# The modular stage of an eleven-stage kernel, rewritten for two batches in the two halves of the array

## The reference, cut to what matters

```python
h = h + _L2_ffn_ref(_layernorm(h, axis=-1), ...)

def _L2_ffn_ref(x, attention_mask, wr, br, w1, b1, w2, b2):
    weights = (jnp.einsum('bsd,do->bso', x, wr) + br)[..., 0]
    k = max(1, int(CAPACITY * s))          # CAPACITY = 0.5
    kk = k - 1 if k > 1 else 1             # 123 of 249 tokens
    _, idx = jax.lax.top_k(weights, k)
    sel_idx = idx[:, :kk]
    sel = take(x, sel_idx)
    h = gelu(sel @ w1 + b1)                # 64 -> 256
    y = (h @ w2 + b2) * w_sel              # 256 -> 64
    return zeros.at[sel_idx].set(y) + x
```

## Time and profile before

| | us |
|---|---|
| median of three runs | 6294.06 |
| the three runs | 6295.24, 6255.51, 6294.06 |
| profiled execution | 6266.99 |
| its span, first to last instruction | 6265.2 |
| PE busy in it | 5338.2 (85%) |
| DVE busy | 3326.5 (53%) |
| ACT busy | 2326.1 (37%) |
| POOL busy | 1796.3 (29%) |
| mean granted PE clock | 0.790 |

### The profile page before, as it was taken

The page is one execution under the profiler, slowest core; times in us unless marked ns, Lnnn a source line. Parts: engine busy times, 40 slices in busy tenths (PEclk is TensorE's granted clock), DMA queues, the critical chain, the costliest instruction groups (busy, mean ns, idle before and its releaser), DMA issues. The chain is left out here.

```text
span 6265.2 us, 119967 instructions
## 1 busy us (share of the span) xinstructions
PE 5338.2 (85%) x34237; PEld 3582.2 (57%) x34237; DVE 3326.5 (53%) x9404; ACT 2326.1 (37%) x5857; POOL 1796.3 (29%) x1988
## 2 busy tenths in 40 slices
PE   4429995677799799997999667887999999979999
PEld 4416663555455466665666564554666666646665
DVE  1245553444455456563444344665777777754554
ACT  3313332000000023333444231113777777755555
POOL 0002221111000134342222472002444444433333
PEclk9997776555555578898999655556999999989999
DMA  0011001111111101013333111110000000013332
GB/s 9 6 36 23 20 21 16 40 39 41 27 25 25 25 20 24 24 25 66 81 81 78 34 42 31 26 27 22 11 10 10 10 10 10 9 28 71 73 73 63
DMA packets 523064, 205.84 MB, mean 33 GB/s; under 512 B 491532, under 2 KB 514044, under 8 KB 522748
## 3 DMA queue, kind: packets, MB, share of 16 engines
q1 hardware_dynamic: 522876, 203.78, 14.7%
HBM read 157.78 MB, written 45.91 MB: 33 GB/s over the span
## 5 line engine op out<-in xcount | busy, mean ns | idle before, releaser
L3026 POOL TENSOR_TENSOR att_P<-att_P,att_rden 125x498 f32<-125x498 f32 x512 | 520.2, 1016 | 640.5 <-DVE att_rden L3297 640.5
L3213 ACT ACTIVATE att_P<-att_pS,att_nb 125x249 f32<-125x249 f32 x1024 | 471.7, 475 | 17.5 <-DVE att_nb L3305 17.5
L2417 DVE TENSOR_TENSOR moe_hT<-moe_silu,moe_pH 128x498 f32<-128x498 f32 x384 | 258.7, 674 | 324.8 <-ACT moe_silu L2403 324.8
L3634 ACT ACTIVATE sw_hT<-sw_pH,sw_b 128x498 f32<-128x498 f32 x512 | 317.9, 672 | 243.2 <-PE sw_pH L3588 243.2
L3129 PEld LDWEIGHTS att_pP<-att_ident,att_P 124*125 124x125 f32 (+1 forms) x2048 | 262.4, 187 | 187.9 <-issue 187.9
L3129 PE MATMUL att_pP<-att_ident,att_P 124*125 124x124 f32 (+1 forms) x2048 | 351.9, 294 | 10.1 <-POOL att_P L3026 8.7
L3305 DVE TENSOR_REDUCE att_nb<-att_pS 125x2 f32<-125x498 f32 x512 | 322.4, 667 | 46.6 <-PE att_pS L3117 45.0
L3220 ACT ACTIVATE att_PTr<-att_pP 125x498 f32<-125x498 f32 x512 | 304.4, 594 | 92.5 <-PE att_pP L3129 86.5
L2403 ACT ACTIVATE moe_silu<-moe_pH 128x498 f32<-128x498 f32 x384 | 225.1, 586 | 285.0 <-PE moe_pH L2360 199.1
L1023 PE MATMUL att_pS<-att_kT,att_qT 16*125 16x249 f32 x1024 | 302.1, 477 | 2.1 <-ACT att_kT L1129 1.3
L3588 PE MATMUL sw_pH<-sw_xT,sw_w 64*128 64x249 f32 x2048 | 286.2, 398 | 0.0
(11 more groups left out here) (456 smaller groups left out, 12609.2 us busy)
## 6 DMA issues: line engine op xcount, KB each, us to landing
moe_share<-mixing SPq DMA_DIRECT2D x64, 498.0 KB
sw_share<-mixing SPq DMA_DIRECT2D x64, 498.0 KB
att_F<-h_stream SPq DMA_DIRECT2D x192, 62.5 KB
att_X<-h_stream SPq DMA_DIRECT2D x192, 62.5 KB
ffn_w<-in_w1b SPq DMA_DIRECT2D x128, 32.5 KB
ffn_w<-in_L_ffn_W SPq DMA_DIRECT2D x128, 32.0 KB
h_stream<-att_H SPq DMA_DIRECT2D x64, 62.5 KB
ffn_F<-h_stream SPq DMA_DIRECT2D x64, 62.5 KB
```

The lines of the kernel that those rows point to most:

```text
L3026: g.tensor_tensor(own, own, bc(rden[:, j % 2, c, :], T), ALU.mult).then_inc(*scaled.one())
L3213: ins = a.activation(P[:, r, c, t, :], pS[:, 2 * r + c, t * T:(t + 1) * T], ACT.Exp, bias=nb[:, r, c, t:t + 1], accum_out=den[:, r, c, t:t ...
L3634: a.activation(hT[:, k % 4, :, :], pH[:, place, :, 0:T], ACT.Relu, bias=b1[:, k:k + 1]).then_inc(*hid_ready.one())
```

## The change

The stage is written anew.

- **Halves.** A pair's two batches lie in partitions 0 to 63 and 64 to 127 (`xT` is 128 x 249). The products with `wr` and `w1` are one matmul for each batch, 64 rows and 249 columns, each in its half of the rows, into different PSUM banks. Two transposes of 128 columns replace four of 64.
- **Second weights still.** `w2` is the stationary operand (128 x 64), `hT` moves (249 columns), and each batch writes its half of the output partitions. The output has channels in the rows, so ACT copies it out with the bias (`yT`), and PE turns it back with two transposes.
- **Biases.** They are added by ACT (`br`, `b1`, `b2`); the ones row and the bias matmuls go.
- **Own weights.** Four transposes of one row and 125 columns of `W` put each token's own weight in its row; DVE copies them out in one instruction.
- **Ranks.** One DVE pass per group, (W - own) > ties, where ties is -tiny for earlier tokens and 0 otherwise, replaces two; one instruction instead of three forms the gate.
- **Normalisation** is `HalfNorm`, POOL adds `xn` and X (`base`) and the result to it (`H1`).
- **Order.** `waves` with three parts (`pre`, `proj`, `main`) and four steps in place of `pipelined`; SP uses `streamed`. There are ten constant transfers instead of eight.

```diff
-        f = Front(st)
...
+        norm = HalfNorm(st, bodies=WAVES)
...
+                streamed(sp, ahead, keep, store, 4)
...
+                def pre(n, u, step):
+                    if step == 0:
+                        g.wait_ge(*xn_ready.before(n))
+                        norm.center(g, n, g4(Fi[:, u, :, :, :]))
+                        norm.square(g, n)
+                    if step == 2:
+                        norm.power(g, n)
+                    if step == 3:
+                        if since(n, 2):
+                            g.wait_ge(*xT_done.after(n - 2))
+                            g.wait_ge(*base_ready.after(n - 2))
+                        norm.scale(g, n, g4(xn[:, u, :, :, :])).then_inc(*xn_ready.one())
+
+                def main(n, u, step):
+                    if step == 1:
+                        g.wait_ge(*kept.after(n, u))
+                        g.wait_ge(*xn_ready.after(n))
+                        g.wait_ge(*h_ready.before(n))
+                        g.tensor_tensor(base[:, :, :], g4(X[:, u, :, :, :]), g4(xn[:, u, :, :, :]), ALU.add).then_inc(
+                            *base_ready.one())
+                    if step == 3:
+                        g.wait_ge(*res_ready.after(n))
+                        g.wait_ge(*base_ready.after(n))
+                        g.wait_ge(*stored.lagging(n, u))
+                        st.held(g)
+                        g.tensor_tensor(g4(H1[:, u, :, :, :]), res[:, :, :], base[:, :, :], ALU.add).then_inc(
+                            *h_ready.one())
...
-                    pe.matmul(pW[:, 0:2 * T], wr[:, :], f.xT[:, u, :, :], start=True, stop=True).then_inc(
-                        *w_done.one())
-                    for k in range(2):
-                        pe.matmul(pH[:, k, 0:2 * T], w1[:, k * 128:(k + 1) * 128], f.xT[:, u, :, :], start=True,
-                                  stop=True).then_inc(*hid_done.one())
...
+                def proj(n, u, step):
                     if step == 0:
...
+                        pe.wait_ge(*xn_ready.after(n))
+                        pe.wait_ge(*xT_ready.before(n))
+                        st.held(pe)
+                        for t in range(2):
+                            ins = pe.transpose(pX[:, t * OFF:t * OFF + ROWS[t]],
+                                               xn[0:ROWS[t], u, t, :, :].rearrange("p b c -> p (b c)"),
+                                               ident[0:ROWS[t], 0:ROWS[t]])
...
+                    if step == 1:
+                        pe.wait_ge(*xT_ready.after(n))
+                        pe.wait_ge(*w_ready.before(n))
+                        pe.wait_ge(*hid_ready.before(n))
...
+                            r = slice(b * C, (b + 1) * C)
+                            ins = pe.matmul(pW[:, b, 0:T], wr[r, :], xT[r, :], start=True, stop=True)
...
+                        for k in range(2):
+                            for b in range(2):
+                                r = slice(b * C, (b + 1) * C)
+                                ins = pe.matmul(pH[:, b, k * T:(k + 1) * T], w1[r, k * 128:(k + 1) * 128], xT[r, :],
+                                                start=True, stop=True)
...
+                def main(n, u, step):
+                    if step == 0:
+                        pe.wait_ge(*w_ready.after(n))
...
+                                ins = pe.transpose(pN[:, g:g + 1], W[0:1, u, b, t * OFF:t * OFF + PT],
+                                                   ident[0:1, 0:1])
...
+                    if step == 1:
+                        pe.wait_ge(*hid_ready.after(n))
+                        pe.wait_ge(*yT_ready.before(n))
...
+                                ins = pe.matmul(pY[b * C:(b + 1) * C, 0:T], w2[:, k, :], hT[:, u, k, b, :],
+                                                start=(k == 0), stop=(k == 1))
...
+                    if step == 2:
+                        pe.wait_ge(*yT_ready.after(n))
...
+                            ins = pe.transpose(pT[:, t * 128:(t + 1) * 128], yT[:, t * OFF:t * OFF + PT], ident[:, :])
...
+                waves(pe, (lambda n, u, step: None, proj, main), STEPS)
...
+                        a.activation(xT[:, :], pX[:, 0:T], ACT.Copy).then_inc(*xT_ready.one())
...
+                        a.activation(W[:, u, :, :], pW[:, :, 0:T], ACT.Identity, bias=br[:, 0:1]).then_inc(
+                            *w_ready.one())
...
+                            ins = a.activation(hT[:, u, k, :, :], pH[:, :, k * T:(k + 1) * T], ACT.Gelu_apprx_tanh,
+                                               bias=b1[:, k:k + 1])
...
+                        a.activation(yT[:, :], pY[:, 0:T], ACT.Identity, bias=b2[:, 0:1]).then_inc(*yT_ready.one())
...
+                        v.tensor_copy(wn[:, :, :].rearrange("p t b -> p (t b)"), pN[:, 0:4]).then_inc(*n_ready.one())
...
+                                v.scalar_tensor_tensor(out=junk[:, b, :], in0=W[:, u, b, :], scalar=wn[:, t, b:b + 1],
+                                                       in1=ties[:, t, :], op0=ALU.subtract, op1=ALU.is_gt,
+                                                       accum_out=count[:, t, b:b + 1]).then_inc(*counted.one())
...
+                        v.scalar_tensor_tensor(gate[:, :], count[:, :, :].rearrange("p t b -> p (t b)"), float(KEEP),
+                                               wn[:, :, :].rearrange("p t b -> p (t b)"), ALU.is_lt,
+                                               ALU.mult).then_inc(*gate_ready.one())
...
+                        v.wait_ge(*turned.after(n))
+                        v.wait_ge(*h_ready.before(n))
+                        v.tensor_tensor(res[:, :, :], pT[:, 0:256].rearrange("p (g c) -> p g c", g=4),
+                                        bc(gate[:, :], C), ALU.mult).then_inc(*res_ready.one())
```

More of the change, by code:

```diff
@@ L2799, in _, with store @@
+                def store(n, u):
+                    sp.wait_ge(*h_ready.after(n))
+                    st.held(sp)
+                    for ins in store_pair(sp, h, H1[:, u, :, :, :], n):
+                        ins.then_inc(*stored.one(u))
+                streamed(sp, ahead, keep, store, 4)
+                for n in (PAIRS - 2, PAIRS - 1):
+                    sp.wait_ge(*stored.after(n, n % 2))
             @block.gpsimd
             def _(g):
-                g.wait_ge(*f.memset_done.after(0))
@@ L2803, in front @@
[L2803 to L2808, removed]
+                g.wait_ge(*memset_done.after(0))
+                def pre(n, u, step):
[10 more added lines that the diff above has]
+                        norm.scale(g, n, g4(xn[:, u, :, :, :])).then_inc(*xn_ready.one())
@@ L2827, in main @@
-                def main(n, u, ahead):
-                    pe.wait_ge(*hid_ready.after(n))
-                    pe.wait_ge(*y_used.before(n))
-                    st.held(pe)
-                    for t in range(2):
-                        for b in range(2):
-                            g = 2 * t + b
-                            pe.matmul(pY[:, g, :], ones[:, :], b2[:, :], start=True, stop=False)
-                            for k in range(2):
-                                ins = pe.matmul(pY[:, g, :], hT[:, u, k, b * T + t * OFF:b * T + t * OFF + PT],
-                                                w2[:, k, :], start=False, stop=(k == 1))
-                    ins.then_inc(*y_done.one())
-                    ahead(0)
-                    ahead(1)
@@ L2859, in _, with main @@
+                def main(n, u, step):
+                    if step == 1:
+                        a.wait_ge(*y_done.after(n))
+                        a.wait_ge(*turned.before(n))
+                        a.activation(yT[:, :], pY[:, 0:T], ACT.Identity, bias=b2[:, 0:1]).then_inc(*yT_ready.one())
+                waves(a, (lambda n, u, step: None, proj, main), STEPS)
             @block.vector
             def _(v):
-                v.memset(ones[:, :], 1.0)
-                f.memsets(v)
-                v.wait_ge(*f.memset_done.after(0))
@@ L2904, in _, with pre @@
-                pipelined(v, front, main, steps=2)
+                v.memset(norm.expo[:, :], -0.5).then_inc(*memset_done.one())
+                v.wait_ge(*const_loaded.after(0))
+                v.wait_ge(*memset_done.after(0))
+                def pre(n, u, step):
+                    if step == 0:
+                        v.wait_ge(*loaded.after(n, u))
+                        norm.sums(v, n, g4(Fi[:, u, :, :, :]))
+                    if step == 2:
+                        norm.spread(v, n, 1e-5)
@@ L2907, in stage_attention3 @@
+                waves(v, (pre, lambda n, u, step: None, main), STEPS)
 def stage_attention3(nc, A, h):
```

208 lines of the change are left out of this document (116 added, 92 removed).

## The result

The kernel after takes **6059.14 us** in the median of four runs (6051.38 to 6068.29), beside 6294.65 for the kernel before in the same comparison: a ratio of 0.9641, interval 0.9600 to 0.9682. I had forecast 6074, with 6005 to 6130 around it. The profiled execution of after is 6064.96, with a span of 6062.6.

The account below looks back on a forecast made before the run. PE was the suspect, on a closed 14.43 us chain per pair. A new 8.0 us slot, with ends, summed to 280.8 us against 484.45, giving 6063, placed at about 6074 for the executions' average; range 6005 to 6130.

Parts of the forecast that it names:

- The chain: Longest closed chain of one slot of `waves`, over PE, `res` on DVE, and POOL: 7.97 us at clock 0.50.
- The 0.14 for the hand-over to `res`: Gap from PE's last transposes to DVE's `res`; with 0.42 for `res` itself, taken as 0.55 us.
- the 0.5 us that the forecast gave back for a late `xT`: In the full-clock slot: chain loses 2.6 us, less 0.5 because `xT` is then late, giving 5.9 us.
- The link through H1: On POOL: H1 of pair s - 2 must precede scaling `xn` of pair s; H1 0.61, scaling 0.69 us later.
- the overlap of the halves: PE's column-half products run beside each other, eight in 1.79 us; rival without overlap: 6198 us, chance 0.04.
- The clock rises: Rival: PE's clock goes to 1.00 in this stage, slot 5.9 us, sum 63 us less, 6011; chance 0.18.
- half of the time there: Form of the clock rival: the stage spends half its time at full clock, total 6042 us.
- The sign that the prediction set: For the stage: the prediction is wrong if PEclk is above 0.7; clock 0.50 was expected over the stretch.
- the stage's sum: Start 9.1 + 1.0, slots 0 and 1 4.5 and 7, thirty slots 240, last slots 7 and 5, end 7.2: 280.8 us.
- The counts: DVE's rank passes: four a slot at 0.48 plus 0.04 us each, 2.1 us, half of before, beside the chain.
- changes of halves cost more: Rival: X lands 5 us later or each change of halves costs 0.37 us; 6104 to 6119 us, chance 0.13.
- the 0.9 us a slot: Extra charge if PE drains at each of four tiling changes a slot, by the skill page; 28 us in the sum.

Follow-up runs that it names:

- the kernel with the fill: The changed kernel with two more whole-array products a slot, read by nobody, ahead of TensorE's wait for `xn`: 5990.81 us, ratio 0.9550.
- the kernel with scaling first: The changed kernel with POOL's scaling moved from step 3 to step 2, ahead of H1 of the pair two before: 6013.24 us, ratio 0.9568.
- the one with padded weights: The changed kernel with `wr`, `w1` and `w2` zero-padded to all 128 rows and columns, so batches cannot run beside each other: 6058.47 us, ratio 0.9631.
- the still weights alone: The kernel before with `w2` stationary in the modular stage and ScalarE's squares moved ahead of its wait for the output products: 6188.64 us, ratio 0.9850.

## Why the prediction was right, and where it was not

**The chain was right, with its price.** The slot at clock 0.50 took 8.17 us, forecast 7.97. Term by term, from the slot's rows above (forecast in brackets): transposes to output products 0.57 (0.50); output products 1.86 (1.79); `wr` 0.99 (0.96); `w1` 1.80 (1.66); last transposes to the start of `res` 0.88 and from there to H1 0.63 (together 1.51; the forecast's 0.79, 0.55 and the hand-over 0.21 make 1.55); H1 to scaling 0.68 (0.61); scaling to the next transposes 0.76 (0.69 and 0.21). The 0.14 for the hand-over to `res` was misread, its own row gives 0.11, and it cost nothing. At clock 1.00 the slot took 5.58 in the kernel with the fill, forecast 5.9. There two errors met: the 0.5 us that the forecast gave back for a late `xT` did not come (its copy ends at 3902.96, the products that need it start at 3903.39), so the chain alone would have been 5.4, and POOL and DVE, which the forecast had beside the chain, put some back. The link through H1 was shown by the kernel with scaling first, the overlap of the halves by the one with padded weights.

**The clock was wrong.** The step that failed is the price of every term at clock 0.50; measured was 0.70 in the full slots. That is the rival *The clock rises*, in the form "half of the time there". The sign that the prediction set, a clock above 0.7, was reached and not passed. The argument against it, that the stage before and the one ahead stay at 0.50 though TensorE is busy 84% and 69% of the time, read the clock off the busy share. The runs show the share to be no guide: 0.50 at 84% in before, 0.70 at 78% in after (156.37 of 200 us), 0.97 at 77% with padded weights (154.83 of 200). The Trainium skill ("TensorE: Matmul & The Clock Gate", Why this matters for your kernels) has it that dense work keeps the full clock and idle gaps lose it; these three do not follow that alone: before works without a break from 4013.79 until the transposes end at 4021.19 and stays at 0.50, and the padded kernel idles 1.65 us in every slot and has 0.97 in the mean. What the padding changed was how much of the array an instruction covers and, with it, that no two run at once; no run tells these apart. The price of the error: (8.17 - 7.32) x 30 = 26 us of stage, against 5 the other way for a slot of 8.17 in place of 8.0.

**The rest of the stage's sum.** The start was short by 2.2 us (12.3 from the first constant to the first sum where I took 10.1): two more constants put off the issue of F by 1.7 us in place of 1, and F then took 6.9 us to its sum where before it took 5.4. Thirty slots took 219.6 in place of 240. What is left, 280.8 + 2.2 - 20.4 - 259.8 = 2.8 us, the slots at both ends took less.

**The counts were wrong and cost nothing.** I took 0.48 + 0.04 us each from the earlier trace rows, a row of a stage in which POOL does nothing but the power, and moved it beside six POOL instructions a slot; it is 0.85. DVE's wait for `pT`, 62.7 us over 31 slots, hides that. At the full clock, where DVE is busy 131.07 of 140 us, there is next to nothing left to hide it; what it costs there no run shows.

**That changes of halves cost more** did not come true: `wr` behind the output products took 0.99 in all. The Trainium skill ("TensorEngine Tiling (Array Packing)", Key Properties) has each change of tiling drain TensorE; the 0.9 us a slot that I had worked out for that did not appear. Nor did X come late.

**The total fits better than its parts.** The forecast was 15 us over, the stage 21 over; the untouched attention stage lay the other way by 19 us in the profiled executions. In the profiled execution, 6064.96, the sum of 6063 is hit to 2 us, and that is luck. Being 15 us off at 6059 is within what that stage does by itself.

**What the prediction did not separate** is which part brings what. It named "shorter PE groups, and an order in which PE need not wait", and the runs give 86 us for the first and 134 for the second, with what is said above on the clock and the order in that 134. The two batches in row halves, as such, seem to have brought little: with two parts in flight everything else of the change gives 394.0, and the still weights alone 398.2, both at 0.50. No run takes the row halves by themselves. Single passes for the ranks brought nothing.

## What to carry to other kernels

Find the closed chain of one slot across all engines' queues and price each link: it gave the slot within 3% at half the clock (the 6% at the full one is in part luck), and its links show where the next gain is (an order swapped on POOL, 38 us). When one engine's group is shortened, look at what its new reader holds up behind it: the squares behind `yT` took 46 of 86 us. And half an array's instructions beside each other may only trade time for clock, as here; look at the granted clock before and after, and where TensorE idles anyway, try whole-array products that nobody reads.

## What the runs showed of the hardware that was not expected

- The granted clock went from 0.70 to 0.97 when the same instructions used all rows and columns (with zeros in them), and to 1.00 with two whole-array products a slot in TensorE's idle time, which took 1.11 us and shortened the slot from 7.32 to 5.58.
- A VectorE pass over two SBUF inputs takes 474 ns with GpSimd idle but for one small instruction a pair and 849 ns beside it, when four follow one another; alternated with passes over one input it takes 501 ns beside the same work. Not explained.
- The order in which instructions for two halves are written within a group made no difference (261.7 and 259.8 us).
- A stage that no kernel touched took 742 us at a granted clock of 0.83 and 806 at 0.75.
